# Layer-0 attention as one sequence of steps, with projections in six parts, maxima units spread by engine time and the output weighed on GpSimd

## What is computed

```python
qkv = h @ Wqkv                                   # 256 -> 768
q = qkv[..., :512].reshape(B, 32, S, 16)         # a plain reshape: head g takes rows of x
k = qkv[..., 512:640].reshape(B, 8, S, 16)       # repeated to 32 heads
v = qkv[..., 640:].reshape(B, 8, S, 16)          # repeated to 16 heads
scores = where(causal, q @ k.T / sqrt(16), -inf)
aw = softmax(scores)
aw = aw[:, :, 0] - lam * aw[:, :, 1]             # pairs of heads
attn = (aw @ v) * (1 - LAMBDA_INIT)
y = (attn @ Wproj), transposed and reshaped, @ Wproj
```

## Time and profile before

| what | us |
|---|---|
| median of 3 runs | 2429.55 (2427.98 to 2432.34) |
| profiled execution | 2430.3 |
| its span | 2428.4 |
| TensorE busy | 2220.2 (91%) |
| VectorE busy | 1829.4 (75%) |
| ScalarE busy | 1547.9 (64%) |
| GpSimd busy | 525.7 (22%) |

### The profile page before, as it was taken

How to read it: one execution, slowest core, us unless ns; L and a number is a source line. 1 busy time by engine, 2 the same in 40 slices (tenths; PEclk the granted TensorE clock), 3 DMA queues, 4 the chain that set the end, 5 groups by cost and what they waited for, 6 DMA issues and landing times. The chain is left out here.

```text
span 2428.4 us, 46606 instructions
## 1 busy us (share of the span) xinstructions
PE 2220.2 (91%) x17772; PEld 992.5 (41%) x17772; DVE 1829.4 (75%) x3782; ACT 1547.9 (64%) x3105; POOL 525.7 (22%) x584
## 2 busy tenths in 40 slices
PE   6799999999999999999999999999999979889984
PEld 4233333333333333333333333334333258567831
DVE  2788888878787888888888888887888348434467
ACT  2167677777767776767676777777767725235633
POOL 2112121303222121212121213131201014100067
PEclk8589999999999999999999999999999979899955
DMA  4120302121121202020303030212100030000001
GB/s 145 36 58 6 66 11 61 22 50 32 41 41 31 47 25 47 30 56 17 66 6 66 6 66 18 55 27 45 32 12 2 2 96 0 1 1 1 1 22 48
DMA packets 95990, 84.79 MB, mean 35 GB/s; under 512 B 48544, under 2 KB 81440, under 8 KB 95776
## 3 DMA queue, kind: packets, MB, share of 16 engines
q1 hardware_dynamic: 95776, 81.91, 15.2%
HBM read 26.81 MB, written 16.78 MB: 18 GB/s over the span
## 5 line engine op out<-in xcount | busy, mean ns | idle before, releaser
L605 DVE TENSOR_REDUCE m_part<-a_bank 128x1 f32<-128x512 f32 (+3 forms) x2560 | 1395.5, 603 | 270.0 <-PE a_bank L906 163.2
L749 ACT ACTIVATE probs<-b_bank 128x512 f32<-128x512 f32 (+1 forms) x2304 | 1173.2, 578 | 412.4 <-PE b_bank L922 407.2
L922 PE MATMUL b_bank<-q_pack,k_pack 34*128 34x512 bf16 (+7 forms) x5120 | 949.0, 348 | 6.2 <-DMA q_pack<-m_rows 1.8
L894 PE MATMUL a_bank<-k_pack,q_pack 64*128 64x512 bf16 (+3 forms) x2560 | 847.2, 357 | 58.5 <-DVE m_part L605 33.0
L960 PE MATMUL acc<-probs,v_tile 128*32 128x512 f32 (+3 forms) x5120 | 587.1, 540 | 22.6 <-ACT o_sb L756 21.5
L922 PEld LDWEIGHTS b_bank<-q_pack,k_pack 34*128 34x128 bf16 (+1 forms) x5120 | 316.5, 94 | 547.7 <-ACT probs L749 392.6
L894 PEld LDWEIGHTS a_bank<-k_pack,q_pack 64*128 64x128 bf16 x2560 | 238.2, 94 | 333.4 <-DVE m_part L605 255.2
L476 POOL TENSOR_SCALAR_AFFINE_SELECT probs<-probs 128x512 f32<-128x512 f32 (+1 forms) x192 | 151.5, 789 | 1019.4 <-ACT probs L749 1019.4
L906 PE MATMUL a_bank<-future,pick 64*128 64x128 bf16 x2048 | 278.3, 219 | 0.0
L906 PEld LDWEIGHTS a_bank<-future,pick 64*128 64x128 bf16 x2048 | 185.7, 96 | 47.5 <-issue 4.7
L960 PEld LDWEIGHTS acc<-probs,v_tile 128*32 128x32 f32 x5120 | 107.3, 108 | 186.6 <-issue 94.2
(11 more groups left out here) (193 smaller groups left out, 1761.0 us busy)
## 6 DMA issues: line engine op xcount, KB each, us to landing
q_pack<-part SPq DMA_DIRECT2D x384, 64.0 KB, 2.3
k_pack<-part SPq DMA_DIRECT2D x192, 64.0 KB, 2.3
scratch<-qkv_row SPq DMA_DIRECT2D x16, 512.0 KB, 2.8
heads<-scratch SPq DMA_DIRECT2D x16, 512.0 KB, 3.7
xg<-in_L_attn_x SPq DMA_DIRECT2D x16, 256.0 KB, 2.8
scratch<-qkv_row SPq DMA_DIRECT2D x32, 128.0 KB, 2.7
q_pack<-m_rows SPq DMA_DIRECT2D x256, 2.0 KB
x<-in_L_attn_x SPq DMA_DIRECT2D x4, 1024.0 KB, 11.7
```

The lines of the kernel that those rows point to most:

```text
L605: dve.tensor_reduce(m_part[:, 2 * hp + side, t, c:c + 1], a_bank[at % A_RING][:, 0:width_a(u % UNITS)], AX.X, ALU.max).then_inc(a_maxed, 1)
L749: act.activation(probs[:, s % P_RING, h, at:C], b_bank[bank_no(("B", par, s, h))][:, at:C], ACT.Exp, scale=HD ** -0.5) \
L894: ins = pe.matmul(a_bank[at % A_RING][:, 0:w], q_pack[buf][rows, hp, 0, q:q + P], k_pack[buf][rows, 0, C * c:C * c + w], start=True, stop= ...
L922: ins = pe.matmul(b_bank[bank_no(slot)][:, at:at + C - q], k_pack[par][rows, n2, P * kt:P * (kt + 1)], q_pack[par][rows, h // 2, n2, C * j ...
```

## The change

1. All groups are one sequence of 576 steps (`LAST_STEP`) and a tail of 3. The last step of a group is like any other: its last two meetings come in steps 0 and 1 of the next group, the copy of `acc` in step 1, the turn in step 2 (`COPY_AT`, `OUTPUT_AT`).
2. The copy of `acc` stands between the second and the third exponential of its step.
3. Projections in six parts of 256 columns, steps 6 to 11; N in step 4. Before the first step they use three banks in turn.
4. `schedule` counts estimated microseconds of TensorE per step (projections and transposes included) against those of VectorE. One unit rides in each half step, the further ones stand at the end of the step behind the transposes and projections; both heads' masks of such a unit alternate. Where a riding unit is narrower than 512 its masks come at once. VectorE negates a block's maxima between the two heads of the next unit. `m_part` is doubled.
5. The output: ScalarE copies the turned bank to `o_rows`, VectorE takes only the reciprocal, GpSimd multiplies by the signs, weighs and adds (`pair`), one step behind the turn. `gather_heads` is on GpSimd (step 14) from group 2 on.

```diff
-MET = 1.1
-FIXED = 64
+WPARTS = 6
+PREP_AT = {4: ("N", 0), **{6 + w: ("W", w) for w in range(WPARTS)}, **{17 + k: ("T", k) for k in range(4)}}
+NORMALISE_AT, DEVIATION_AT, CENTRE_AT, GATHER_AT, SPLIT_AT = 0, 1, 3, 14, 22
+GATES_AT = 24
+TENSOR_TIME = {"N": 0.75, "W": 1.26, "T": 0.77, "O": 0.80}
+VECTOR_TIME = {NORMALISE_AT: 1.5, CENTRE_AT: 0.9}
 
 
 def schedule():
 
-    met = [[s - LAG] if s < STEPS - 1 else range(STEPS - 1 - LAG, STEPS) for s in range(STEPS)]
-    b_cost = [sum(widths(s)) + (MET * sum(sum(widths(m)) for m in met[s] if m >= 0)) for s in range(STEPS)]
-    a_cost = [width_a(u % UNITS) + FIXED for u in range(LEAD, LEAD + UNITS)]
-    ends, b_done, a_done, k = [], 0, 0, 0
+
+    vector = [2 * (width_a(u % UNITS) / 960 + 0.065) for u in range(LEAD, LEAD + UNITS)]
+    outputs = [(last + LAG + 1) % STEPS for last in J_LAST]
+    tensor = [1.30 * sum(widths(s)) / C + 0.87 * sum(widths(s - LAG)) / C + 0.2
+              + (TENSOR_TIME[PREP_AT[s][0]] if s in PREP_AT else 0) + (TENSOR_TIME["O"] if s in outputs else 0)
+              for s in range(STEPS)]
+    all_vector = sum(vector) + sum(VECTOR_TIME.values())
+    ends, done, other, k = [], 0, 0, 0
     for s in range(STEPS):
-        b_done += b_cost[s]
-        while k < UNITS and a_done + a_cost[k] / 2 < sum(a_cost) * b_done / sum(b_cost):
-            a_done += a_cost[k]
+        other += VECTOR_TIME.get(s, 0)
+        while k < UNITS and done + other + vector[k] / 2 < all_vector * sum(tensor[:s + 1]) / sum(tensor):
+            done += vector[k]
             k += 1
         ends.append(k)
     return ends[:-1] + [UNITS]
...
+def units_by(n):
+
+    g, s = n // STEPS, n % STEPS
+    return min(LEAD + UNITS * g + ENDS[s], UNITS * GROUPS) if n >= 0 else LEAD
+
+
+def units(n):
+
+    return range(units_by(n - 1), units_by(n))
+
+
+LAST_STEP = STEPS * GROUPS
 NEXT = [j for j in range(NJ) if A_LAST[j] < LEAD]
-PREP_AT = {7: "N", 8: "W0", 9: "W1", 10: "W2", 11: "W3", 17: "T0", 18: "T1", 19: "T2", 20: "T3"}
-MISC = {s: [n for n in ([f"M{M_AT[s]}"] if s in M_AT else []) + ([f"O{O_AT[s]}"] if s in O_AT else [])
-            + ([PREP_AT[s]] if s in PREP_AT else [])] for s in range(STEPS)}
-PREP = tuple(PREP_AT.values())
-
-
-def uses_of(par, last):
-
+COPY_AT = {STEPS * g + J_LAST[j] + LAG: 4 * g + j for g in range(GROUPS) for j in range(NJ)}
+OUTPUT_AT = {n + 1: block for n, block in COPY_AT.items()}
+MAXIMA_AT = {n + 2: 4 * (u // UNITS) + A_LAST.index(u % UNITS)
+             for n in range(LAST_STEP) for u in units(n) if u % UNITS in A_LAST}
+
+
+def uses_at(n):
+
+    g, s = n // STEPS, n % STEPS
     out = []
-    for s in range(STEPS):
-        for u in MISC.get(s, []):
-            if last and (u in PREP or (par == 1 and u in [f"M{j}" for j in NEXT])):
-                continue
-            out.append((s, u))
+    if n in MAXIMA_AT:
+        out.append(("M", MAXIMA_AT[n]))
+    if n in OUTPUT_AT:
+        out.append(("O", OUTPUT_AT[n]))
+    if s in PREP_AT and g + 2 < GROUPS:
+        what, k = PREP_AT[s]
+        out.append((what, {"N": 1, "W": WPARTS, "T": 4}[what] * (g + 2) + k))
     return out
 
 
-GATES_AT = 24
-
-
-SLOTS = [slot for par in range(2) for s in range(STEPS)
-         for slot in [("B", par, s, h) for h in range(QH)] + [(use, par, s, 0) for use in MISC[s]]]
-SLOTS[-1:-1] = [None] * (-len(SLOTS) % B_RING)
...
+            def pair(n):
+
+                g, j = n // NJ, n % NJ
+                o = o_sc[:, :].rearrange("p (t h e) -> p t h e", t=TB, h=QH)
+                halves = o_sc[:, :].rearrange("p (t a c e) -> p t a c e", t=TB, a=2, c=2)
+                dst = attn[:, g, TB * j:TB * (j + 1), :].rearrange("p t (a e) -> p t a e", a=2)
+                pool.wait_ge(o_inverted, n + 1)
+                if n == 0:
+                    pool.wait_ge(lam_step, 7)
+                if n:
+                    pool.wait_ge(o_added, n)
+                pool.tensor_tensor(o_w[:, :, :], o_rl[:, :, :], signs[:, :, :], ALU.mult).then_inc(o_weighed, 1)
+                pool.wait_ge(o_weighed, n + 1)
+                pool.tensor_tensor(o, o_rows[:, :].rearrange("p (t h e) -> p t h e", t=TB, h=QH)[:, :, :, 0:HD],
+                                   o_w[:, :, :].unsqueeze(3).broadcast_to([P, TB, QH, HD]), ALU.mult).then_inc(o_scaled, 1)
+                pool.wait_ge(o_scaled, n + 1)
+                pool.tensor_tensor(dst, halves[:, :, :, 0, :], halves[:, :, :, 1, :], ALU.add).then_inc(o_added, 1)
+
+            for n in range(TAIL):
+                g, s = n // STEPS, n % STEPS
+                if g + 2 < GROUPS and s == DEVIATION_AT:
+                    inverse_deviation(g + 2)
+                if s in DIAG and n < LAST_STEP:
+                    mask(n)
+                if n - 1 in OUTPUT_AT:
+                    pair(OUTPUT_AT[n - 1])
+                if g + 2 < GROUPS:
+                    if s == GATHER_AT:
+                        gather_heads(g + 2)
+                    if s == SPLIT_AT:
+                        split(g + 2)
+            pair(NJ * GROUPS - 1)
 
         @block.vector
...
+            def unit_maxima(u, last):
+
+
+                m = NJ * (u // UNITS) + A_LAST.index(u % UNITS) if u % UNITS in A_LAST else None
+                before = NJ * ((u - 1) // UNITS) + A_LAST.index((u - 1) % UNITS) if u and (u - 1) % UNITS in A_LAST else None
+                maximum(u, 0)
+                if before is not None:
+                    negate(before)
+                maximum(u, 1)
+                if before is not None:
+                    negate_rest(before)
+                if m is not None:
+                    block_maximum(u, m)
+                    if last:
+                        negate(m)
+                        negate_rest(m)
+
+            def invert(n):
+
+                dve.wait_ge(o_taken, n + 1)
+                if n:
+                    dve.wait_ge(o_scaled, n)
+                dve.reciprocal(o_rl[:, :, :], o_rows[:, :].rearrange("p (t h e) -> p t h e", t=TB, h=QH)[:, :, :, HD]) \
+                    .then_inc(o_inverted, 1)
 
...
+            for n in range(TAIL):
+                g, s = n // STEPS, n % STEPS
+                ahead = list(units(n)) if n < LAST_STEP else []
+                for k, u in enumerate(ahead):
+                    unit_maxima(u, u == UNITS * GROUPS - 1)
+                    if k == 0 and n - 1 in OUTPUT_AT:
+                        invert(OUTPUT_AT[n - 1])
+                if not ahead and n - 1 in OUTPUT_AT:
+                    invert(OUTPUT_AT[n - 1])
+                if g == GROUPS - 1 and s == GATES_AT:
+                    gates()
+                if g + 2 < GROUPS:
+                    if s == NORMALISE_AT:
+                        normalise(g + 2)
+                    if s == CENTRE_AT:
+                        centre(g + 2)
+            invert(NJ * GROUPS - 1)
...
+            def take_output(block):
+                act.wait_ge(pv_done, START + STEPS * (block // NJ) + J_LAST[block % NJ] + 1)
+                if block:
+                    act.wait_ge(o_taken, block)
+                act.activation(o_sb[:, :], acc[:, :], ACT.Copy).then_inc(acc_copied, 1)
+
+            def take_rows_of_output(block, no, bank):
+                act.wait_ge(misc_filled, no)
+                if block:
+                    act.wait_ge(o_added, block)
+                act.activation(o_rows[:, :], bank[:, :], ACT.Copy).then_inc(o_taken, 1)
+
+            for n in range(TAIL):
                 for h in range(QH):
+                    if n < LAST_STEP:
+                        exponential(n, h)
+                    if h == 1 and n in COPY_AT:
+                        take_output(COPY_AT[n])
...
+            def project(n, w, bank):
+                r, a = w // 3, D * (w % 3)
+                if w == 0 and n == 0:
                     pe.wait_ge(wqkv_in, 16)
                 if w == 0:
-                    pe.wait_ge(hT_ready, upto(2 * n + 2))
+                    pe.wait_ge(hT_ready, 2 * n + 2)
                 for k in range(2):
-                    ins = pe.matmul(misc[:, 0:b - a], hT[:, k, P * r:P * (r + 1)], wqkv[:, k, a:b], start=k == 0, stop=k == 1)
+                    ins = pe.matmul(bank[:, 0:D], hT[:, k, P * r:P * (r + 1)], wqkv[:, k, a:a + D], start=k == 0, stop=k == 1)
                 ins.then_inc(misc_filled, 1)
 
...
+            def two_heads(n, hp, u):
+
+
+                short = u is not None and width_a(u % UNITS) < C
+                score(n, 2 * hp, 0)
                 if u is not None:
+                    unit_head(u, 0)
+                if short:
+                    mask_head(u, 0, 0)
+                    mask_head(u, 0, 1)
+                score(n, 2 * hp, 1)
+                if u is not None and not short:
+                    mask_head(u, 0, 0)
+                    mask_head(u, 0, 1)
+                score(n, 2 * hp + 1, 0)
                 if u is not None:
+                    unit_head(u, 1)
+                score(n, 2 * hp + 1, 1)
                 if u is not None:
```

(30 more changed lines are left out.)

418 lines of the change are left out of this document (134 added, 284 removed).

## The result

Four runs of the changed kernel have a median of 2409.48 us (2407.45 to 2413.69), four of the kernel before beside them 2429.69: the ratio is 0.9918, 95% interval [0.9901, 0.9935]. It is faster, by 20 us where 2330 us had been predicted (-100) and 2284 to 2368 as the range. The sign was right and four fifths of the gain are missing. Steps and groups are those of the text before the prediction: steps of a group are counted from 0, the first group is group 1.

What follows compares the result with a forecast made beforehand. TensorE, 91% busy, was taken as the bound, with 12.9 us of waits in a 114.9 us group. Terms summed to -6.2 a group (108.7), -94 in all: 2336, rounded to 2330 us; likeliest range 2302 to 2360, 8-in-10 range 2284 to 2368.

Steps and rivals of the forecast that it cites:

- part 7: GpSimd takes the gather and two output multiplications: some 6 us more work a group, nobody waiting, no cost.
- part 4: Maxima units spread by engine time, with less VectorE work: VectorE's waits fall from 7.7 to 3.8, -3.9 us a group.
- a group over 113: Sign on group length: over 113 us would mean wrong at the root; about 108.5 was expected.
- part 1: Group boundary, steps 35 to 3: without the flush its waits go, -3.5 us a group.
- part 2: Copy of acc moved between second and third exponential: the next block's first meeting stops waiting, -1.7 us a group.
- 3 six projections: Projections in six 256-column parts: +0.4 us a group on TensorE, +0.3 on ScalarE beside other work.
- Part 5: Step 10: pack starts later, so block 2's rows of maxima land at +32.9; new wait +1.0 us, between 0 and 2.
- Part 6: Step 22: first_part in ScalarE's queue delays exponentials, so TensorE waits for its bank: +1.5 us, between 0 and 2.
- if GpSimd stood among TensorE's releasers: Sign in TensorE's timeline: waits released by GpSimd would mean the prediction was wrong at the root.
- 0.4 for each of four steps with four units: Wait of heads for the ring of three banks in four-unit steps, within a 2.8 us sum for ring waits.
- rival A: VectorE's waits stay because the three-bank ring, not the share per step, stalls TensorE: group 112.6, 2391 us; chance 0.17.
- 4 or more: Sign at the fifteenth group's step 10: first matmul waits 4 us or more for its rows of maxima.

Runs made afterwards that it cites:

- e5: Changed kernel with GpSimd's split queued in step 26 and held by a semaphore until block 1's maxima are negated; 2377.26 us, ratio 0.9779.
- e10: e5 with at most three units of the maxima in any one step; 2352.23 us, ratio 0.9673.
- e12: e5 with the flush at the group's end put back; 2407.01 us, ratio 0.9895.
- e6: Kernel before with the copy of acc put behind the second exponential, except in a group's last step; 2424.69 us, ratio 0.9976.
- e7: Changed kernel with the copy of acc back behind all four exponentials; 2421.62 us, ratio 0.9962.
- e14: e13 with the projections in four parts of 512 and 256 columns instead of six; 2348.44 us, ratio 0.9657.
- e13: Changed kernel with at most three units a step and the split in twelve GpSimd instructions of 512 columns; 2351.74 us, ratio 0.9676.
- e3: Changed kernel with each VectorE maximum reduction reading only half of its columns; 2333.27 us, ratio 0.9590.
- e4: Kernel before with each VectorE maximum reduction reading only half of its columns; 2325.64 us, ratio 0.9565.
- e9: e5 with the units of the maxima spread by columns, as in the kernel before; 2404.90 us, ratio 0.9892.

## Why the prediction was wrong

Two steps of it failed: part 7, which put GpSimd's effect on VectorE at nothing, and part 4, which was more than twice too large. Part 7 alone does not explain the miss: without the collision the kernel takes 2377 us (e5), still above the range; with the bunches capped too it takes 2352 (e10), inside it. The prediction's own line for being wrong at the root, a group over 113, was passed.

Terms in us a group; measured ones are differences of groups whose clock stayed at 1.00.

| part | predicted | measured | by |
|---|---|---|---|
| 1 no flush | -3.5 | -2.7, an estimate | e12 against e5, and a row of before |
| 2 copy of acc, steps 5 and 23 | -1.7 | -0.8 to -1.0 | e6; e7's steps 5 and 23 |
| 3 six projections | +0.4 | +0.38 | e14 against e13 |
| 4 units by engine time, VectorE's lighter load | -3.9 | -1.7 | e3 and e4 against their wholes |
| 5 SyncE's queue | +1.0 | 0 | no wait in the first fourteen groups |
| 6 ScalarE behind first_part | +1.5 | 0.5 seen | trace, below |
| 7 GpSimd, "nobody waiting" | 0 | +1.9, and +0.7 by the clock | e5 against the change |
| sum | -6.2 | -1.6, and +0.7 by the clock | traces |

The single terms make -2.7 - 0.8 + 0.4 - 1.7 + 0.5 + 1.9 = -2.4, against 113.31 - 114.88 = -1.57 measured. So 0.8 us is unassigned. The half reductions narrow it down: there parts 1, 2, 3, 5 and 6 together brought 1.9, where their single terms make 2.6. The gap lies among these, and parts 4 and 7 close with them: -1.9 - 1.7 + 2.0 = -1.6.

**Part 7 failed, and with the clock it is the largest error, 2.6 us a group.** I had the row: 0.91 us for a product of 16 numbers beside the split. I read it as a price of that product, which the change takes off VectorE, and concluded that GpSimd works "with nobody waiting". I asked what GpSimd's added work would do, and not which other small instruction of VectorE would fall beside the split that was already there once the steps moved. The kernel before had the sign of this too: its negations (L615) have a mean of 342 ns, since one in four takes 0.76 beside a mask of 1.1 us that ends with it. The row was in the trace and in none of my groups:

```profile
1000.70 0.76 DVE L615 TENSOR_SCALAR m_neg<-m_max 128x16 bf16<-128x16 f32 x1
```
```profile
1000.33 1.10 POOL L476 TENSOR_SCALAR_AFFINE_SELECT probs<-probs 128x1024 f32<-128x1024 f32 x1 [3.64 <-ACT probs L749]
```

The rule that I cited from the Trainium skill (SBUF — State Buffer, "Who interferes with whom") names more than I used: the same section counts a `tensor_scalar` from SBUF among the operations that can take the port pair VectorE shares with GpSimd, and says the one that issues first keeps it for its whole instruction. By that rule the trace agrees: the 2.26 us is a `tensor_scalar`, the 4.04, 3.03 and 1.57 are instructions with two SBUF inputs, each ends with GpSimd's running instruction, and reductions are untouched. The prediction's own sign, "if GpSimd stood among TensorE's releasers", did not show it either: TensorE's releaser is VectorE, and VectorE is busy. In the profile the wait looks like work.

**Part 4 was mis-sized, 1.7 of 3.9.** The "0.4 for each of four steps with four units" was too small: e10 shows that the bunches cost 1.6 us a group more than the same units at three a step. And the 1.7 is the whole part, VectorE's lighter load included; e9 against e5 shows that the spread alone shortens no wait for VectorE (279 us against 254), so that its mechanism, a share per step that VectorE can follow, is not shown. In step 8 TensorE has done three heads of its last two units behind a projection and waits 0.57 us for the fourth's bank:

```profile
954.48 0.60 PE L877 MATMUL a_bank<-k_pack,q_pack 64*128 64x512 bf16 x3
955.65 0.39 PE L877 MATMUL a_bank<-k_pack,q_pack 64*128 64x512 bf16 x1 [0.57 <-DVE m_part L591]
```

A bunch of four units is eight heads for three banks. With the bunches gone part 4 would be -3.3, close to its forecast. This is rival A's mechanism (the ring, not the share per step) for half of the term.

**Parts 1 and 2 were right in kind and too large**, 3.5 for 2.7 and 1.7 for 0.8 to 1.0. I took all that steps 35 to 3 lasted over their price as the flush's. They went from 15.6 to 11.8 us, but with six units in them where there had been nine, so this doesn't show part 1's size. In part 2 I took both delays of a meeting as the group's loss; in the kernel before, step 24 gives back 0.65 of it (e6).

**Part 5's mechanism was right to 0.3 us, and its wait did not come.** The rows land at +33.2 (e9), 32.9 by the forecast; but the new spread puts 18 units into steps 5 to 10, where the old one has 14, and TensorE comes at +33.7. Where the old spread brings it there earlier, it waits, twice a group. What I booked as a loss beside a gain was one thing: the new spread's early bunches fill the time in which the DMA lands. The fifteenth group, without projections, shows what part 5 said of it, a wait of "4 or more": 3.7 us for the same rows at its step 10, and the clock falls to 0.50 with it. The group takes 109.0 us against 108.4 before, where I had 3 less. TensorE:

```profile
1756.39 0.60 PE L908 MATMUL b_bank<-q_pack,k_pack 64*128 64x512 bf16 x1 [3.70 <-DMA q_pack<-m_rows]
```

**Part 6** shows in step 21 or 22 as forecast, at a third of its size. TensorE, then ScalarE:

```profile
1001.12 0.39 PE L908 MATMUL b_bank<-q_pack,k_pack 64*128 64x512 bf16 x1 [0.52 <-ACT probs L740]
```
```profile
998.67 1.91 ACT L712 ACTIVATE part<-headT 80x2048 bf16<-80x2048 f32 x1
```

Outside the fourteen groups the first step came 1.8 us earlier (127.6 against 129.4; 3 forecast), and the last group with the stages behind it took 0.6 us more.

So in a group whose clock stayed at 1.00, 4.6 of the 6.2 us are missing: 1.9 for VectorE's wait behind GpSimd at a moment nobody had fixed, 2.2 for part 4, and 0.5 for the rest. That the rest is so small is luck: parts 1 and 2 brought 1.7 less than forecast and 0.8 is unassigned, while parts 5 and 6 cost 2.0 less. The clock takes another 0.7 on average.

## What to carry to other kernels

A short VectorE instruction whose mean is several times that of its fastest was, in every case here, waiting inside, and no idle time shows it: look beside it for a long GpSimd instruction, and list every small one that may fall there once steps move. Cut the long instruction into pieces (it cost 1.3 us of GpSimd a group and gave 36 us, 2.5 of them before the first step), or tie it behind the short ones; a step number in a queue without a wait fixes no moment. When spreading producers over a ring of three banks, cap the bunch as well as the average.

## What the runs showed of the hardware

- The length of VectorE's wait was what was left of GpSimd's running instruction: 16 elements a partition took 0.17 to 4.04 us (every instruction of VectorE shown here as held is this small). With GpSimd's pieces of 1.16 us the negations took at most 0.61 in the steady groups.
- Reductions from the banks and a reciprocal ran at their usual length beside the same instructions.
- One pause of TensorE of 1.16 us, in step 26, was followed by a granted clock of 0.50 in six groups of the same kernel and not in the other eight; four of the six were 1.34 us longer; in the eighth group the mean clock was 0.50 from 1016 to 1018 and 0.87 from 1018 to 1020.
- On GpSimd the product of 256 elements takes 0.62 us, the one of 16 0.22 and the sum of 128 0.46, against 0.42 for the 256 on VectorE.
